# A two-stage kernel: side work of the attention stage placed by half slots, and the gate product in halves

## The reference, cut to what matters

```python
xc = conv(xn @ W_in)                     # 4 taps
alpha = exp(-8 * softplus(base) * sigmoid(forget))
beta = sqrt(1.0 - alpha ** 2 + 1e-06)
h = linear_recurrence(alpha, beta * sigmoid(inp) * xc)
x = x + gelu(gate) * h @ W_out.T
x = x + gelu(mgate) * mx @ W_shrink.T    # then a routed expert layer with a capacity
```

## Time and profile before

| | us |
|---|---|
| median of 3 runs | 1431.36 (1431.35 to 1436.4) |
| the profiled execution itself | 1437.65 |
| its span, first to last instruction | 1435.9 |
| busy in the span: PE, DVE | 1220.5, 1160.6 |
| busy in the span: ACT, POOL | 968.2, 824.6 |
| mean granted TensorE clock | 0.943 of full speed |

### The profile page before, as it was taken

How to read it: one execution, slowest core, us unless ns; L and a number is a source line. 1 busy time by engine, 2 the same in 40 slices (tenths; PEclk the granted TensorE clock), 3 DMA queues, 4 the chain that set the end, 5 groups by cost and what they waited for, 6 DMA issues and landing times.

```text
span 1435.9 us, 26041 instructions
## 1 busy us (share of the span) xinstructions
PE 1220.5 (85%) x8624; PEld 492.4 (34%) x8624; DVE 1160.6 (81%) x2518; ACT 968.2 (67%) x1653; POOL 824.6 (57%) x1068
## 2 busy tenths in 40 slices
PE   1499899899899999999999999856999899899853
PEld 0123233233233233233233223323545545545533
DVE  2668889889889889889989988433789889889874
ACT  1177777777777777877877878555767667666630
POOL 5303554654654654655555444634677877877763
PEclk7589999999999999999999989888999999999975
DMA  1121101101101101101100100000000000000000
GB/s 56 50 83 42 35 31 42 36 31 41 37 31 42 37 31 40 38 30 41 39 30 32 34 14 3 1 0 1 1 8 16 8 8 16 8 8 16 8 8 22
DMA packets 52517, 37.87 MB, mean 26 GB/s; under 512 B 8864, under 2 KB 51744, under 8 KB 52384
## 3 DMA queue, kind: packets, MB, share of 16 engines
q1 hardware_dynamic: 52384, 36.22, 7.9%
HBM read 6.31 MB, written 4.19 MB: 7 GB/s over the span
## 4 chain that ended last, share of the span: by engine, by line
PE 33%; DVE 23%; POOL 20%; issue 13%; SPq 5%; ACT 5%; POOLq 0%; DMA 0%; ACTq 0%; DVEq 0%
DVE neg_max L473 11%; PE bank L201 10%; PE bank L182 9%; SPq L621 4%; PE bank_pair L169 4%; ACT probs L348 3%; PE bank L210 3%; POOL probs L1154 2%; PE bank L272 2%; POOL x_all L1148 2%; POOL zn L1146 1%; POOL rs_t L1088 1%; POOL probs L1119 1%; POOL rs_x L1088 1%; POOL rs_h L1116 1%
## 5 line engine op out<-in xcount | busy, mean ns | idle before, releaser
L473 DVE TENSOR_REDUCE neg_max<-bank_pair 128x2 f32<-128x1024 f32 x512 | 615.5, 1215 | 120.7 <-PE bank_pair L169 115.9
L348 ACT ACTIVATE probs<-bank 128x512 f32<-128x512 f32 x1024 | 558.5, 596 | 113.2 <-PE bank L182 108.6
L182 PE MATMUL bank<-q_stack,k_stack 50*128 50x512 bf16 x1024 | 362.3, 390 | 36.4 <-ACT probs L348 19.3
L201 PE MATMUL bank<-probs,v_pad 128*32 128x256 f32 x4096 | 331.4, 396 | 2.7 <-ACT outT L306 2.3
L169 PE MATMUL bank_pair<-k_stack,q_stack 48*128 48x512 bf16 x1024 | 293.8, 397 | 31.0 <-DMA k_stack<-k_parts 15.7
L182 PEld LDWEIGHTS bank<-q_stack,k_stack 50*128 50x128 bf16 x1024 | 83.6, 93 | 301.2 <-ACT probs L348 228.6
L201 PEld LDWEIGHTS bank<-probs,v_pad 128*32 128x32 f32 x4096 | 81.1, 108 | 175.6 <-issue 156.0
L724 PE MATMUL bank_pair<-probs,w_gates 128*128 128x512 f32 x256 | 122.7, 624 | 16.7 <-DVE probs L1046 8.9
L522 POOL TENSOR_TENSOR f_b<-f_bf,ffn_bias 128x512 bf16<-128x512 bf16 x16 | 18.9, 1182 | 157.3 <-ACT f_bf L353 157.3
L169 PEld LDWEIGHTS bank_pair<-k_stack,q_stack 48*128 48x128 bf16 x1024 | 54.0, 94 | 60.5 <-DVE neg_max L473 41.2
L1154 POOL TENSOR_TENSOR probs<-probs 128x1024 f32<-128x1024 f32 x16 | 37.7, 2354 | 62.9 <-DVE probs L1068 62.9
(11 more groups left out here) (232 smaller groups left out, 2252.6 us busy)
## 6 DMA issues: line engine op xcount, KB each, us to landing
q_stack<-q_parts SPq DMA_DIRECT2D x384, 32.0 KB
k_stack<-k_parts SPq DMA_DIRECT2D x384, 32.0 KB
x_all<-in_z_dram SPq DMA_DIRECT2D x16, 256.0 KB, 2.8
out_dram<-x_all SPq DMA_DIRECT2D x16, 256.0 KB, 2.3
q_stack<-max_rows SPq DMA_DIRECT2D x64, 8.0 KB
w_gates<-in_w_gates_dram SPq DMA_DIRECT2D x1, 512.0 KB, 3.7
w_in<-in_w_in_dram SPq DMA_DIRECT2D x1, 256.0 KB, 2.7
w_grow<-in_w_grow_dram SPq DMA_DIRECT2D x1, 256.0 KB, 3.8
```

Of the source, the lines that this page charges most:

```text
L182: nc.tensor.matmul(st_ps[h][:, :], k_stack[par][rows, p, c * P:(c + 1) * P], q_stack[par][rows, p, :], start=True, stop=True).then_inc(s[" ...
L201: mm = nc.tensor.matmul(acc[32 * g:32 * g + 32, cols], v_pad[bpar][:, kc, 4 * a + g, :], probs[:, at + g, cols], start=(t == 0 and kc == 0 ...
L348: nc.scalar.activation(probs[:, 4 * (n % RING) + g, :], st_ps[g % 2][:, :], ACT.Exp, scale=SCALE)\
L473: nc.vector.tensor_reduce(neg_max[j // 4][:, c, j % 4, :], score_ps[c % 2][:, :, :], AX_X, ALU.max, negate=True).then_inc(s["max_read"], 1)
```

## The change

Attention: all side work is placed by half slot u. TensorE's proj, v, q and k products are cut into two pieces in neighbouring half slots; ScalarE reads either `between` the two exponentials of a half slot or `behind` them; VectorE has at most one piece of side work behind each reduce. The order of the `misc` bank, of GpSimd's blocks and of SP's copies changes with it. L1: GpSimd's gate product is written in two halves, stands in the next iteration behind part of that iteration's roots, and the w_out product takes each half as it comes; one minus the square of alpha moves from GpSimd to a ScalarE Copy with scale -1 and bias 1; Sqrt stands ahead of both Gelus, and the explicit preload of the Gelu table is dropped. The diff, cut:

```diff
-    MISC = [yT, ffn, o1, v, oT, proj, maxT1, znT, q, k, o0, maxT0]
+    MISC = [o1, oT, proj, maxT1, yT, ffn, v, znT, q, k, maxT0, o0]
...
+        def side_product(u):
+            if u == 3 and live(i, -1):
                 out_nat(1, i - 1)
+            if u == 6 and live(i, -1):                       # oT
+            if u in (8, 9) and live(i, -1):
+                tokens("proj", oT, w["proj"], (0, 1) if u == 8 else (2, 3), s["proj_ps"])
+            if u == 15 and live(i, -2):                      # yT
+            if u == 16 and live(i, -2):
+                tokens("ffn", yT, w["ffn"], range(C), s["ffn_ps"])
+            if u in (17, 18) and live(i, 1):
+                tokens("v", znT, w["v"], (0, 1) if u == 17 else (2, 3), s["v_ps"])
+            if u == 19 and live(i, 2):                       # znT
+            for n, first in (("q", 21), ("k", 25)):
+                if u in (first, first + 1) and live(i, 2):
+                    features(n, u - first)
+            if u == 31 and live(i, 0):
+                out_nat(0, i)
...
+        def between(u):      # ScalarE, behind the first exponential of u
+            7: oT   17: f_bf   19: v (t=1)   20: znT   23: q hi   24: q rest   27: k hi   28: k rest
+        def behind(u):       # ScalarE, behind the second
+            1: outT1   13: max_rows(1, i)   15: yT   17: outT0   18: v (t=0)   29: max_rows(0, i+1)
...
+        def behind(u):       # VectorE, behind the reduce of u
+            0, 2, 8: y_absmax, y_absmax, poison   4: divide(1)   10: att   11: split_max(1)
+            12, 13: stats b   14, 15: stats a   18, 19: stats c   21, 22: stats d
+            24, 25, 26, 28, 30: y_grid, y_grid, y_sum, y_q, y_absmax   27: split_max(0)   31: divide(0)
...
     def pool(gp, i, par):    # blocks in this order
-        zn(i+2), f_b(i-2), z_res(i-1), x2(i-2), x1(i-1), split q, split k (i+2), y(i-1)
+        z_res(i-1), zn(i+2), x1(i-1), f_b(i-2), y(i-1), split q, split k (i+2), x2(i-2)
...
     def sync(sp, i, par):
         load_x(sp, i + 3)
-        stack q1, k1 (i+1); max_rows_out(1, 0); stack q0, k0 (i+2); max_rows_out(0, 1)
+        stack q1 (i+1); max_rows_out(1, 0); stack k1 (i+1); stack q0 (i+2); max_rows_out(0, 1); stack k0 (i+2)
...
     # L1, TensorE
-            wait(pe, s["gh_ready"], b + 1)
             wait(pe, s["xh_ready"], b)
-            natural(bank_o, gh, w["out"], s["wout_ps"])
+            for k in range(2):
+                wait(pe, s["gh_ready"], 2 * b + k + 1)
+                for c in range(C):
+                    mm = nc.tensor.matmul(bank_o[:, c * D:(c + 1) * D], gh[:, k, c * P:(c + 1) * P], w["out"][:, k, :],
+                                          start=(k == 0 and c == 0), stop=(k == 1), skip_group_check=True)
+            mm.then_inc(s["wout_ps"], 1)
...
     # L1, ScalarE
             A(beta, alpha, ACT.Square).then_inc(s["sq_ready"], 1)
+            wait(act, s["sq_ready"], b + 1)
+            A(beta, beta, ACT.Copy, bias=1.0, scale=-1.0).then_inc(s["om_ready"], 1)
...
-            nc.scalar.preload_act_table_set("gelu_and_others")
...
+        if live(i, -1):
+            A(beta, beta, ACT.Sqrt, bias=consts["tiny"][:, 0:1]).then_inc(s["beta_ready"], 1)
         if live(i, -2):
             A(grown, pair1[:, :, :], ACT.Gelu).then_inc(s["mg_ready"], 1)
-        if live(i, -1):
-            A(beta, beta, ACT.Sqrt, bias=consts["tiny"][:, 0:1]).then_inc(s["beta_ready"], 1)
...
     # L1, GpSimd
             TT(r[:, 1, :], r[:, 0, :], half_neg, ALU.pow).then_inc(q, 1)
+        if live(i, -2):
+            b = i - 2
+            wait_apart(gp, s["h_ready"], 2 * (b + 1), past_wait)
+            wait_apart(gp, s["gate_ready"], b + 1, past_wait)
+            wait_apart(gp, s["wout_ps"], b, past_wait)
+            for n in range(2):
+                TT(gh[:, n, :], h[:, n, :], gate_g[par][:, n, :], ALU.mult).then_inc(s["gh_ready"], 1)
...
-            TS(beta, beta, -1.0, 1.0, ALU.mult, ALU.add).then_inc(s["om_ready"], 1)
...
-            TT(gh, h, gate_g[(par + 1) & 1], ALU.mult).then_inc(s["gh_ready"], 1)     # the block at the end
```

More of the change, by code:

```diff
@@ L319, in side_read, with read_hi @@
-            if slot == 4 and live(i, -1):
+            src = misc[:, :].rearrange("p (cu t g d) -> p cu t g d", t=2, g=4, d=HD)
+            dst = v_pad[1 - par][:, :, :, :].rearrange("p c (u t g) e -> p (c u) t g e", u=2, t=2)
+            nc.scalar.activation(dst[:, :, t, :, 16 * t:16 * t + HD], src[:, :, t], ACT.Copy).then_inc(s["v_ready"], 1)
+        def read_hi(n, parts):
+            wait(act, s[n + "_ps"], i + 2 + 1)
+            for half in range(2):
+                wait(act, s[f"{n}{half}_ready"], 16 * STACK_DMAS * (i + 2))
+            nc.scalar.activation(parts[:, 0, :], bank_of(n, i)[:, :], ACT.Copy).then_inc(s[n + "_hi"], 1)
@@ L320, in side_read, with read_all @@
+        def read_all(n, rest):
+            wait(act, s[n + "_lo"], 3 * (i + 2))
+            nc.scalar.activation(rest[:, :], bank_of(n, i)[:, :], ACT.Copy).then_inc(s[n + "_hi"], 1)
+        def between(u):
+            if u == 7 and live(i, -1):
                 wait(act, s["oT_ps"], i - 1 + 1)
@@ L322, in side_read @@
                 nc.scalar.activation(oT[:, :], misc[:, :], ACT.Copy).then_inc(s["oT_ready"], 1)
-            if slot == 6 and live(i, 2):
+            if u == 17 and live(i, -2):
+                wait(act, s["ffn_ps"], i - 2 + 1)
+                wait(act, s["ffn_biased"], i - 2)
+                nc.scalar.activation(f_bf[:, :, :].rearrange("p c d -> p (c d)"), misc[:, :], ACT.Identity,
+                                     bias=0.0, scale=consts["s_both"][:, 0:1]).then_inc(s["ffn_read"], 1)
+            if u == 19 and live(i, 1):
+                read_v(1)
+            if u == 20 and live(i, 2):
                 wait(act, s["znT_ps"], i + 2 + 1)
@@ L349, in scalar @@
                         .then_inc(s["exp_done"], 1)
-                if (slot, g) == (2, 1) and live(i, -2):
-                    wait(act, s["ffn_ps"], i - 2 + 1)
-                    wait(act, s["ffn_biased"], i - 2)
-                    nc.scalar.activation(f_bf[:, :, :].rearrange("p c d -> p (c d)"), misc[:, :], ACT.Identity,
-                                         bias=0.0, scale=consts["s_both"][:, 0:1]).then_inc(s["ffn_read"], 1)
-            side_read(slot)
+                (behind if g % 2 else between)(u)
     def vector(dve, i, par):
@@ L436, in between @@
                     .then_inc(q, 1)
-            if slot == 2 and live(i, -2):
-                b = i - 2
+            if u == 2 and live(i, -2):
                 wait(dve, q, 9 * b + 6)
@@ L441, in between @@
                     .then_inc(q, 2)
-            if slot == 3 and live(i, -2):
-                b = i - 2
+            if u == 8 and live(i, -2):
                 wait(dve, q, 9 * b + 8)
@@ L446, in between @@
                 nc.vector.tensor_scalar(poison[:, :], y_absmax[:, :], 1e30, None, ALU.mult).then_inc(q, 1)
-            if slot == 6 and live(i, -1):
-                b = i - 1
+            if u == 21 and live(i, -2):
+                wait(dve, s["ffn_biased"], b + 1)
+                raw_stats(nc, bn_d, lambda c: f_b[:, c, :], s["stat_d_raw"], C)
+            b = i - 1
+            if u == 4 and live(i, -1):
+                divide(1, b)
+            if u == 10 and live(i, -1):
                 wait(dve, s["proj_ps"], b + 1)
@@ L455, in between @@
                     .then_inc(s["att_ready"], 1)
-            if slot == 10 and live(i, -1):
-                b = i - 1
+            if u == 11 and live(i, 0):
+                split_max(1, i)
+            if u == 12 and live(i, -1):
+                wait(dve, s["att_ready"], b + 1)
+                wait(dve, s["x1_step"], 8 * b)
+                raw_stats(nc, bn_b, lambda c: att[:, c, :], s["stat_b_raw"], C)
+            if u == 14 and live(i, 3):
+                wait(dve, x_loaded, 16 * (i + 3 + 1))
+                wait(dve, s["prep_step"], 9 * (i + 3))
+                raw_stats(nc, bn_a, lambda c: x_all[:, i + 3, c * D:(c + 1) * D], s["stat_a_raw"], C)
+            if u == 18 and live(i, -1):
                 wait(dve, s["x1_step"], 8 * (b + 1))
@@ L474, in vector @@
                                             negate=True).then_inc(s["max_read"], 1)
-                (side if c % 2 else between)(2 * p + c // 2)
+                behind(C * p + c)
     def first_stats(dve):
```

398 lines of the change are left out of this document (181 added, 217 removed).

## The result

The changed kernel takes 1419.07 us (median) against 1431.49 for the kernel before in the same comparison: a ratio of 0.990, 95% interval 0.9875 to 0.9929, so 12.4 us faster where I had forecast 35. A second comparison gave 1417.68 and 0.992 (0.989 to 0.994). The time lies inside my range; the gain is about a third of the forecast.

What follows compares the result with a forecast made beforehand. Attention was taken as bound by a two-buffer ring of transposes and exponentials with side work paid serially. Start -5, attention -34, seam 0, L1 +6, tail -2 sum to -35, taken from the median: 1396 us, range 1370 to 1428.

Steps and rivals of the forecast that it cites:

- Attention, the mechanism: Attention batch: side products and reads, paid one after the other, overlap once spaced; 53.6 to 51.0 us, thirteen batches -34.
- the slower rival: Attention slots 0 and 8 wait for late maximum rows; a batch takes 55.2 us, total 1451; chance 0.08.
- The start: First attention slots: rows no longer wait behind 12 k copies, but v, znT and q move later; -5 us.
- Halved products cost one more issue each, below 0.1 us: Attention's side products on TensorE: cutting each in two adds only one issue, below 0.1 us.
- The last two attention batches gain about 1.5: End of the attention stage, counted within the seam: the last two batches get about 1.5 us shorter.
- seam 0: Attention to L1: x1 and y earlier -1.3, Copy +1.0, roots before gh(0) +2, last batches gain 1.5; net 0.
- L1 (b): L1, one minus square moved to ScalarE: gains a Copy of 1.0, loses a load of 1.28, within slack; 0.
- (c): L1, Sqrt ahead of Gelu: 3.7 us before Gelu of mg, mx waits; TensorE's 2.4 idle leaves 0 to 0.3 loss.
- (a): L1, GpSimd: roots fill the wait for scans, gh starts 1.3 later, halves give 1.0 back; net 0.
- (d): L1, roots beside the scans: contention makes scans up to 0.95 us longer, once or twice; taken as +0.3.
- The iteration in sum, +0.5: L1 terms together: +0.5 us an iteration, for about 13 full ones +6, bounds -9 and +21.
- The tail, -2: End of the kernel: with no roots left, the last two gate products hand on halves 1 us earlier each; -2.

Runs made afterwards that it cites:

- the last experiment: New attention with whole side products and the L1 of before, with SP's copies of k ahead of the maximum rows again: 1539.0 us, ratio 1.074.
- the two profiles above: Second profile of the unedited kernel before (median 1432.2 us), and the profile of the new attention stage with the L1 of before (1407.2 us).
- the whole products: Changed kernel with proj, v, q and k products whole again, each at the half slot of its second half: 1411.7 us, ratio 0.986.
- the attention part: Attention stage of the change with the L1 stage of the kernel before: 1407.2 us, ratio 0.984.
- three kernels: Table load put back in ScalarE's gap: changed kernel (Sqrt table) 1411.2; with Gelu of mg first 1410.4; new attention with only L1's halves 1406.7 us.
- the L1 part: L1 stage of the change with the attention stage of the kernel before: 1441.2 us, ratio 1.008.

## Why the prediction was right and wrong

**Attention, the mechanism: right.** I had put the loss down to products and reads paid one after the other, and the cure to distance. VectorE's waits for a score pair fell from 5.0 to 3.0 us, and a batch takes 51.41 where I had walked 51.0 and taken 53.6 to 48.3 as bounds. TensorE's waits for rows are 0.3 us a batch, so the late rows of the slower rival did not come; the last experiment shows how near they are.

**The start: right in sum** (-4.8 us at the first copy of outT in batch 1 in the two profiles above, -3 to -6 in other pairs; forecast -5).

**"Halved products cost one more issue each, below 0.1 us": wrong.** A half is 0.7 us where half of the whole is 0.58, eight times a batch, some of it where VectorE waits for TensorE. Measured by the whole products: 6 us in all, 0.41 a batch. With them a batch takes the 51.0 that I had walked for the halves.

**"The last two attention batches gain about 1.5", seam 0: wrong.** They lose 5.9 (97.2 for 91.3): 2.2 to 3.5 for the placement, the rest for a fall of the clock that the profile of before lacks. I carried the gain of a full batch over to batches whose side work is missing. In the kernel before these batches were already short (48.5 without the fall of the clock, and 42.8), and no row of mine showed them. This (7.4 against the forecast), 1.3 us between the last copy and L1's first x4 addition, and the halving (13 times 0.41) are some 14 of the 15 us between my -39 and the -24 of the attention part.

**L1 (b), "ScalarE gains a Copy of 1.0 and loses one load of 1.28": wrong, the largest error that one line undoes.** The dropped line didn't take a load away, it moved one: out of ScalarE's wait for the convolution and onto the path conv copies, Sqrt, Gelu of mg, mx. It is worth 6.5 to 7.9 us, in two of three kernels ahead of and behind the steady iterations and not in them. The path was in my own text: under (c) I counted a load, Sqrt and a load in front of the Gelu, and let TensorE's 2.4 us of idle time an iteration cover them. That idle time was spent twice, since the roots of (a) lean on it too: with the load out of the way w_out waited 1.80 us for the gate product behind them. And a term is missing: the wait for the Gelu came out as walked (2.38 us), but the clock that falls behind it in every second iteration, 0.6 us each time (27.6 for 27.0), I had put at nothing.

The Trainium skill, page ScalarE: Activation LUTs, section Table sets: the hidden batching unit, has the rule to batch calls by table set. The change follows it: with Sqrt ahead of both Gelus the trace has three loads an iteration for four. The time rose all the same, as the load that was dropped had been free and one of those that stayed was not. The section What ACT_TABLE_LOAD costs of the same page gives 2.66 us with the drain; here a load is 1.28 us and the next instruction starts 0.01 to 0.02 behind it (1137.13 and 1138.42 above), and the measurement decides.

**L1 (a), roots in front, net 0: wrong**, 0.44 us an iteration at the full clock (27.01 for 26.57). It is hidden in the whole change and shown without the load's loss: 5 us with the Copy on ScalarE (1410.4 for 1405.3), 22 without. I had filled GpSimd's wait, and what stood behind the wait, w_out, now waits for the filling. **(d), +0.3 for scans beside the roots: not seen on VectorE.** The pair of scans takes 3.29 as it did before; the root pays, 1.93 beside the scans for 1.02 alone. The Trainium skill, page SBUF — State Buffer, section Who interferes with whom, has a VectorE instruction with two SBUF inputs contend with a GpSimd instruction that reads SBUF. The trace agrees: 3.29 for 2.34 in the earlier trace rows, and the root's 1.93 for 1.02. **One minus square on ScalarE, 0: right by itself** (1405.3 for 1406.7), and 8 us to the good in the changed kernel. **The iteration in sum, +0.5: right in size by luck.** It is +0.6 to +0.7 (27.3 and 27.4 for 26.7), but not from the scans: 0.3 are there at the full clock (27.01), the rest is the clock. **The tail, -2: not seen:** three of the last iterations took 67.95 us with the L1 part and 68.02 with that of before (attention part alone).

**The seam, for L1's edits +3 (1.0 and 2): too small.** The L1 part was 5.6 late there, its early iterations included. With the Sqrt table's load in the gap the changed kernel is 3.9 us shorter in this stretch (139.6 for 143.5), so much of it goes with the dropped line; the rest I did not take apart.

**The result in sum.** L1's part measured +10 for +4, attention -24 for -39, and these 21 us are nearly all of the 23 between 1396 and 1419. Taking the saving from the median and not from the profiled execution was right: that execution had the fall of the clock in batch 14.

Undoing the Sqrt order or the roots one at a time gave nothing, though the roots were worth 5 us once the load was back in the gap. Each was covered by another limit: the load on ScalarE's path, the gate product on GpSimd's, and the clock, which fell more often in both of these kernels. A mean over iterations did not show it; the iterations at the full clock did.

## What to carry to other kernels

A load, a copy or an issue that runs while its engine waits cost nothing here; before dropping or merging it, ask where the next one will run. Idle time of the bound engine covers one delay only: list all that lean on it, and price what the clock may do behind a new wait. When an edit is undone and the mean stays, look at single iterations before calling it worthless. And a period's gain holds for full periods; cost the first and last ones from their own rows.

## What the runs showed that was not expected

TensorE's granted clock falls from 1.00 to 0.50 (2.4 to 1.2 GHz) after light stretches inside the steady work: after 2.69 busy of 4 us in batch 14, and in L1 after waits of 1.8 to 2.4 us, where single iterations grow from 27.0 to 27.6 or 28.6. Behind the same wait it falls in one iteration and not in the next, and in batch 14 in one execution and not in the other; that fall is 3.7 of the 3.8 us between the two profiled executions of before. The rest of the spread of 10 us was not profiled.

Half of a product isn't half of its time: 512 columns of v, proj, q or k are 1.12 to 1.16 us, 256 are 0.68 to 0.71.

A wrong order of twelve 0.7 us issues on a queue that is never the busiest engine cost 138.6 us, the largest effect in this study.
